# A local attention product split by halves of the queries, and element work moved to ScalarE and GpSimd

## The chip, the cores and the metric

The kernel runs on one core of a Trainium2 chip. Its time is the device time of one execution in microseconds. Five engines work at once and wait for each other by semaphores: TensorE (PE, with its weight loads shown as PEld), VectorE (DVE), ScalarE (ACT), GpSimd (POOL) and SyncE (SP), which issues DMAs.

## What is computed

The reference takes 8 batches of 1024 tokens with 256 features and does, for each batch:

```
h  = layernorm(x) * (1 + scale) + shift                      # adaLN, from the conditioning vector
q,k,v = block-diagonal projections of h (16 heads of 16), q and k rotated
y  = causal softmax(q k^T / 16) v                            # one head of 256 features, 1024 keys
x  = x + gate * y;   u = layernorm(x) * (1 + scale) + shift
for 2 layers:                                                # local transformer
    qkv = shift_token(u) @ wqkv                              # 8 heads of 64
    q,k = l2norm, scale, rotary;  windows of 128 queries look at their own and the last window,
          masked to keys j with i-128 <= j <= i
    u = u + softmax(q k^T * 8) v @ wo
    h = layernorm(shift_token(u)) @ w1 + b1;  u = u + (a * gelu(g)) @ w2 + b2
out = x + gate2 * u
```

## The kernel before, in words

Everything of a batch stays in SBUF. The first attention (pieces `st` to `ys`) works on 8 tiles of 128 tokens; the local layers work on 8 windows `w` of 128 tokens, two layers, so a batch has 16 windows, numbered `n` over all batches (128 in all); the feed-forward part works on two halves `g` of 512 tokens in 5 blocks and a tail of 42 columns.

The work is cut into about 9,000 named pieces. Each engine executes its pieces in an order read from tables: `BEGIN` gives a begin time to each piece of one batch, batch `b` is put `b * PERIOD` later, `EDGE` has other times for the first batch and `ONCE` those of the weight preparation. `schedule()` sorts the pieces of each engine by these times. `plan_banks()` then gives the eight PSUM banks to the pieces in PE's order, and a piece that takes over a bank waits until the piece before has been read out. The begin times set the order and the banks and nothing else: at run time each piece starts when its engine has come to it and its semaphores allow it.

The pieces that the change touches:

- **G** (line 547) are the scores of a window, one piece for each half `f` of the heads: fp32 matmuls with 64 rows of the array and 64 columns (the profile writes 64*64), so that four work at a time.
- **H** (line 565) transposes the probabilities with 64 rows and 128 columns (64*128). The 192 keys of 64 queries lie in `PW` between stretches of 64 zeros; H reads 256 keys for each query, and so the transposed probabilities `PTW` hold two blocks of 64 by 64 zeros for each head. The zeros are written once for each batch, by GpSimd in piece `pz` (lines 1353 and 1354).
- **I** (line 581) is the product with V, one piece for each `f`: for two pairs of heads and for the old and the new 128 keys, two fp32 matmuls side by side, each with 128 rows, 64 columns (128*64) and 128 queries moving. Both keys' halves accumulate in the same place of one bank. Each fp32 matmul is two instructions in the trace, so a piece is 16 of them (8 in the first window of a layer, which has no old keys).
- `oh` (ACT, line 837) and `ol` (DVE, line 1130) copy the product out as two fp16 parts, and **J** (lines 594 and 598) multiplies it by `wo` with the whole array (128*128).
- `rw` (DVE, line 936) applies the first layer norm, `x` minus the mean times the inverse deviation, two tiles at a time; `af` (DVE, line 950) applies scale and shift to the transposed tiles in PSUM; `lk` (DVE, lines 1158 and 1160) is the layer norm before the feed-forward part, four instructions for two windows. Their inverse deviations come from GpSimd: `rt` and `lt` call `root` (lines 294 and 296), an addition and a power.
- `yr` (DVE, line 1183) adds the feed-forward result to `U`; in the last layer it also multiplies by the gate and adds `X` (lines 1188 and 1190), which ends the window. SyncE stores it and loads the next batch's tiles into `X`, after which `st` (line 920) starts the next batch.

Around the change, the largest PE pieces are E (lines 508 and 514, the qkv projection, fp16, 128*128), Wg and Wa (613, 617), Y (160 to 162, 638), the scores and products of the first attention (461, 160 to 162) and the fp32 transposes F (524), D and N (407), pp (419).

Of the kernel before, what the change touches and what calls it, by code (L numbers as in the profile page):

```python
# [22 lines left out]
P = 128  # L23
# [5 lines left out]
AH = 16  # L29
# [17 lines left out]
def adaln_kernel(nc, x, w_q, w_k, w_v, wqkv, q_scale, k_scale, wo, ln_g, ln_b, w1, b1, w2, b2,  # L47
# [3 lines left out]
    with ExitStack() as ctx:  # L51
# [38 lines left out]
        mx1, nm1, sm1, ri1 = (stats[:, 0, :, 16 + i] for i in range(4))  # L90

# [96 lines left out]
        s_pz, s_pa = sem("prob_pads_zero"), sem("odd_probs_normalised")  # L188
# [103 lines left out]
        def root(pool, ve, mv, rs, lo, hi, s_eps, count):  # L292

            pool.tensor_scalar(ve[:, lo:hi], mv[:, lo:hi, 1], EPS, None, ALU.add).then_inc(s_eps, 1)  # L294
            pool.wait_ge(s_eps, count)
            return pool.tensor_tensor(rs[:, lo:hi], ve[:, lo:hi], neg_half[:, 0:hi - lo], ALU.pow)


        block = nc.Block()
        with block:  # L300
# [100 lines left out]
            def _(pe):  # L401
# [9 lines left out]
                for piece in ORDER["pe"]:  # L411
# [141 lines left out]
                    elif k == "H":  # L553
# [3 lines left out]
                        if n % (DEPTH * NT) == 0:  # L557
                            pe.wait_ge(s_pz, n // (DEPTH * NT) + 1)
# [9 lines left out]
                    elif k == "I":  # L568
# [7 lines left out]
                        bk = bank["I", n]  # L576
                        for i in range(2):
# [115 lines left out]
            def _(act):  # L693
                for piece in ORDER["act"]:
                    k, ids = piece[0], piece[1:]
                    if k == "hh":
# [5 lines left out]
                        act.activation(ht[0][:, :, 1 + p * 256:1 + (p + 1) * 256], hf1[:, p % 2], ACT.Copy).then_inc(s_hh, 1)  # L702
                    elif k == "vc":
# [117 lines left out]
                    elif k == "hc":  # L821
                        n, f = ids
                        act.wait_ge(s_ht, at("H", n, f))
                        if n >= 1:
                            act.wait_ge(s_pv, at("I", n - 1, f))
                        c = 1 if n % NT else 2
# [3 lines left out]
                    elif k == "oh":  # L830
# [6 lines left out]
                        act.activation(ot[0][:, :, :], ps[:, bank["I", n], :].rearrange("p (h n) -> p h n", h=4),  # L837
# [75 lines left out]
            def _(dve):  # L913
                for piece in ORDER["dve"]:
# [11 lines left out]
                    elif k == "rw":  # L926
                        b, p = ids
                        dve.wait_ge(s_rstd, at("rt", b, p))
                        if p >= 2:
                            dve.wait_ge(s_xnT, at("pp", b, p - 2))  # L930
                        elif b:
                            for s in range(2):
                                dve.wait_ge(s_ft, at("F", last_n(b), s))
                        for i in range(2):
                            t = 2 * p + i
                            last = dve.tensor_scalar(
                                xn1[:, p % 2, i, :, :].rearrange("p c (h q) -> p (c h) q", q=AD),
                                X[:, t, :].rearrange("p (q h) -> p h q", h=AH),
                                mv1[:, t, 0:1], rs1[:, t:t + 1], ALU.subtract, ALU.mult)
                        last.then_inc(s_xn, 1)  # L940
                    elif k == "af":
                        b, p = ids
                        dve.wait_ge(s_xnT, at("pp", b, p))
                        if p >= 2:
                            dve.wait_ge(s_hl, at("hl", b, p - 2))
                        if b == 0 and p == 0:
                            dve.wait_ge(s_modc, 1)
                        bk = bank["pp", b, p]
                        for c in range(NC):
                            last = dve.tensor_scalar(hf1[:, p % 2, c, :], ps[:, bk, c * 256:(c + 1) * 256],  # L950
                                                     modc_all[:, b, NC + c:NC + c + 1], modc_all[:, b, c:c + 1],
                                                     ALU.mult, ALU.add)
                        last.then_inc(s_hf, 1)
# [134 lines left out]
                    elif k == "tm":  # L1088
# [4 lines left out]
                        dve.wait_ge(s_rinv, at("pw", n))  # L1093
                        if n < 2:
                            dve.wait_ge(s_masks, 1)
# [22 lines left out]
                    elif k == "hv":  # L1118
                        n, f = ids
                        dve.wait_ge(s_ht, at("H", n, f))  # L1120
                        if n >= 1:
                            dve.wait_ge(s_pv, at("I", n - 1, f))
                        c = 1 if n % NT else 2
# [3 lines left out]
                    elif k == "ol":  # L1127
                        n, = ids
                        dve.wait_ge(s_oh, at("oh", n))
                        dve.tensor_tensor(ot[1][:, :, :], ps[:, bank["I", n], :].rearrange("p (h n) -> p h n", h=4),  # L1130
                                          ot[0][:, :, :], ALU.subtract).then_inc(s_ol, 1)
# [19 lines left out]
                    elif k == "lk":  # L1151
                        L, p = ids
                        dve.wait_ge(s_lnr, at("lt", L, p))
                        if L or p >= 2:
                            dve.wait_ge(s_nt, at("N", *divmod(L * 4 + p - 2, 4)))
# [765 lines left out]
```

## Time and profile before

| | us |
|---|---|
| median of 3 timed runs | 2636.95 (2635.13 to 2637.11) |
| span of the profiled execution | 2634.1 |
| PE busy | 2526.7 (96%) |
| DVE busy | 2260.9 (86%) |
| ACT busy | 1935.6 (73%) |
| POOL busy | 1303.7 (49%) |

The profile gives the profiled execution's own time as its span, from the first to the last instruction; the timed runs also hold what lies around the span, some 3 us. A matmul's record lasts until its result is out of the array, so records of matmuls that follow each other overlap, and the distance between their starts is what they cost. A busy PE is therefore not a PE at its peak.

### The profile page before, as it was taken

How to read it: one execution, taken by the hardware profiler on the slowest of the kernel's cores; microseconds unless marked ns; L12 is line 12 of the kernel's file. 1: busy time of each engine (PE TensorE's matmuls, PEld its weight loads, DVE VectorE, ACT ScalarE, POOL GpSimd, SP SyncE). 2: the span in 40 equal slices, each digit the busy share in tenths (PEclk: the TensorE clock that was granted, in tenths of full speed). 3: DMA queues.
4: the chain of work that ended last, by engine and by line, in shares of the span. 5: the costliest groups of instructions: out<-in, count | busy, mean ns of one | idle time of the engine just before them, and what ended most of it. 6: DMA issues, size and time to landing. Idle time of an engine off the chain costs nothing.

```text
span 2634.1 us, 71297 instructions
## 1 busy us (share of the span) xinstructions
PE 2526.7 (96%) x25566; PEld 1725.1 (65%) x25566; DVE 2260.9 (86%) x6247; ACT 1935.6 (73%) x4782; POOL 1303.7 (49%) x953
## 2 busy tenths in 40 slices
PE   7899989999899998999999999999999999999998
PEld 4566666666567665676656666666766666666675
DVE  8997889878898788987889878998889978799785
ACT  3698856888478784788748787587874878658884
POOL 2364535555355554555436554365544555446552
PEclk8999999999999999999999999999999999999999
DMA  5000010000100000000000000000000000000000
GB/s 192 22 7 8 5 43 3 9 5 15 33 3 9 6 17 30 4 10 4 18 29 5 8 5 20 25 6 8 6 19 25 6 8 6 20 25 6 7 6 21
DMA packets 51021, 46.45 MB, mean 18 GB/s; under 512 B 11530, under 2 KB 47980, under 8 KB 50548
## 3 DMA queue, kind: packets, MB, share of 16 engines
q1 hardware_dynamic: 50004, 40.78, 5.0%
q8 instruction: 213, 3.49, 0.6%
q14 instruction: 132, 1.08, 0.1%
q10 hardware_dynamic: 672, 1.10, 0.1%
HBM read 25.06 MB, written 8.42 MB: 13 GB/s over the span
## 4 chain that ended last, share of the span: by engine, by line
PE 69%; DVE 12%; ACT 8%; issue 5%; POOL 4%; DMA 1%; SPq 1%; DVEq 0%; POOLq 0%; ACTq 0%
PE ps L508 10%; PE ps L613 9%; PE ps L581 8%; PE ps L547 6%; PE ps L514 5%; PE ps L617 4%; PE ps L565 4%; PE ps L524 3%; PE ps L594 3%; PE ps L160 2%; PE ps L162 2%; PE ps L161 2%; ACT ar_b L808 2%; PE ps L461 2%; PE ps L407 2%
## 5 line engine op out<-in xcount | busy, mean ns | idle before, releaser
L808 ACT ACTIVATE ar_b<-ar_b,small 128x192 f32<-128x192 f32 (+1 forms) x1024 | 445.2, 437 | 50.4 <-DVE small L1100 48.6
L1366 POOL TENSOR_TENSOR small<-small,neg_half 128x16 f32<-128x16 f32 x128 | 382.2, 2986 | 121.8 <-DVE small L1059 119.9
L1370 POOL TENSOR_TENSOR ar_c<-ar_c 128x1024 f32<-128x1024 f32 x128 | 302.7, 2365 | 282.3 <-DVE ar_c L1086 281.7
L1100 DVE CUSTOM_DVE_ANT_0 ar_b<-ps,mask_t,small 128x192 f32<-128x192 f32 x896 | 319.3, 413 | 29.7 <-PE ps L547 29.2
L1385 POOL TENSOR_TENSOR mlp<-mlp 128x512 f16<-128x512 f32 x160 | 196.3, 1231 | 200.5 <-ACT mlp L863 199.3
L508 PE MATMUL ps<-wqkv_hi,ht_hi 128*128 128x512 f16 x768 | 292.2, 381 | 0.0
L508 PE MATMUL ps<-wqkv_lo,ht_hi 128*128 128x512 f16 x768 | 291.1, 379 | 0.0
L613 PE MATMUL ps<-ht_hi,w_hi 128*128 128x512 f16 (+1 forms) x704 | 268.2, 381 | 5.5 <-ACT ht_hi L759 5.5
L613 PE MATMUL ps<-ht_hi,w_lo 128*128 128x512 f16 (+1 forms) x704 | 267.1, 379 | 0.0
L581 PE MATMUL ps<-ar_b,ar_a 128*64 128x128 f32 x3840 | 239.4, 276 | 0.5 <-DVE ar_b L1124 0.3
L294 POOL TENSOR_SCALAR stats<-stats 128x2 f32<-128x2 f32 x128 | 33.2, 260 | 407.6 <-DVE stats L1149 312.5
L514 PE MATMUL ps<-wqkv_hi,ht_lo 128*128 128x512 f16 x768 | 228.4, 379 | 0.0
L581 PEld LDWEIGHTS ps<-ar_b,ar_a 128*64 128x64 f32 x3840 | 207.2, 137 | 29.7 <-issue 17.4
L617 PE MATMUL ps<-ht_lo,w_hi 128*128 128x512 f16 (+1 forms) x704 | 209.9, 380 | 0.0
L1176 DVE SCALAR_TENSOR_TENSOR mlp<-ps,bias,mlp 128x512 f32<-128x512 f32 x192 | 142.5, 749 | 70.1 <-PE ps L617 33.1
L819 ACT ACTIVATE ar_b<-ar_b,rsw 128x192 f32<-128x192 f32 (+1 forms) x512 | 193.7, 441 | 11.2 <-DVE rsw L1111 10.2
L547 PE MATMUL ps<-ar_a 64*64 64x64 f32 (+2 forms) x5536 | 196.7, 282 | 2.8 <-ACT ar_a L798 2.8
L1124 DVE COPY ar_b<-ps 128x512 f32<-128x512 f32 (+1 forms) x256 | 160.2, 648 | 44.1 <-PE ps L565 44.1
L808 ACT ACTIVATION_READ_ACCUMULATOR ar_b<-ar_b,small 128x1 f32 x1024 | 193.4, 189 | 0.0
L547 PEld LDWEIGHTS ps<-ar_a 64*64 64x64 f32 x5536 | 153.4, 133 | 40.0 <-issue 22.6
L160 PE MATMUL ps<-w_hi,mlp 128*128 128x256 f16 x640 | 175.4, 274 | 0.2 <-POOL mlp L1385 0.2
L162 PE MATMUL ps<-w_hi,mlp 128*128 128x256 f16 x640 | 175.1, 274 | 0.0
(193 smaller groups left out, 6673.3 us busy)
## 6 DMA issues: line engine op xcount, KB each, us to landing
xu<-in_L_attn_x_dram SPq DMA_DIRECT2D x32, 256.0 KB, 2.8
out_dram<-xu SPq DMA_DIRECT2D x64, 128.0 KB, 2.4
rows<-xu SPq DMA_DIRECT2D x128, 63.5 KB
mlp<-in_L_ffn_wqkv_dram SPq DMA_DIRECT2D x2, 1536.0 KB, 6.4
modb<-mod_rows SPq DMA_DIRECT2D x8, 384.0 KB, 4.5
rows<-in_L_ffn_w_dram SPq DMA_DIRECT2D x2, 1364.0 KB, 9.5
rows<-xu SPq DMA_DIRECT2D x112, 0.5 KB
ar_b<-in_L_wmod_dram SPq DMA_DIRECT2D x2, 768.0 KB, 7.4
```

The costliest lines, as they stand in the source:

```text
L160: pe.matmul(o, a[0], b[0], start=start, stop=False)
L162: return pe.matmul(o, a[1], b[0], start=False, stop=stop)
L508: pe.matmul(ps[:, bk, :], ht[0][:, c, a:a + P], wqkv_p[i][:, L % DEPTH, c, s * INNER:(s + 1) * INNER], start=(c == 0 and i == 0), stop=False)
L514: last = pe.matmul(ps[:, bk, :], ht[1][:, c, a:a + P], wqkv_p[0][:, L % DEPTH, c, s * INNER:(s + 1) * INNER], start=False, stop=(c == 1))
L547: last = pe.matmul(ps[HQ * half:HQ * half + HQ, bk[q], i * KW + o:i * KW + o + m], QT[r:r + HQ, n % 2, hp, HQ * half:HQ * half + HQ], KT[r ...
L581: last = pe.matmul(ps[64 * q:64 * q + 64, bk, (h // 2) * P:(h // 2 + 1) * P], V[:, (n - 1 + kb) % 4, h * DH:(h + 1) * DH], PTW[:, f, q, 2 ...
L613: pe.matmul(ps[0:m, bk, :], q[:, L % DEPTH, c, 2 * j + i, 0:m], ht[0][:, c, a:a + 512], start=(c == 0 and q is w1_p[0]), stop=False)
L617: last = pe.matmul(ps[0:m, bk, :], w1_p[0][:, L % DEPTH, c, 2 * j + i, 0:m], ht[1][:, c, a:a + 512], start=False, stop=(c == 1))
L808: last = act.activation(pw, pw, ACT.Exp, bias=mnw[:, n % 2, h:h + 1], scale=-1.0, accum_out=smw[:, n % 2, h:h + 1])
L1100: dve.tensor_tensor_reduce(out=PW[:, pw_at(f, q, i) + c:pw_at(f, q, i) + KW], in0=ps[:, bk, i * KW + c:(i + 1) * KW], in1=mask, scale=rinv ...
L1366: pool.tensor_tensor(rinv[:, n % 4, :], ssm[:, n % 2, :], neg_half[:, 0:16], ALU.pow).then_inc(s_rinv, 1)
L1370: pool.tensor_tensor(M1[:, n % 2, :], M1[:, n % 2, :], M2, ALU.add).then_inc(s_add, 1)
```

## The change

1. **The V product.** Piece I no longer multiplies the zero blocks. Each head's queries are two halves of 64, accumulated in two adjacent banks. For each pair of heads it issues: the old 128 keys for the first half, two matmuls side by side (128 rows, 64 columns, 64 queries moving); the new 128 keys for the second half, two such; and then the remaining 64 keys of each half, four matmuls with 64 rows and 64 columns. In a layer's first window the old keys fall out. `oh` and `ol` read both banks, `plan_banks` gives I two banks, piece `pz` is gone, and the first window's copies `hc` and `hv` wait for the first attention's last product instead, and its `tm` for the last transposes.
2. **Moves.** `rw`, `af` and `lk` run on ScalarE, as one activation for each former DVE instruction, `Identity` with scale and bias from SBUF. For that the mean times the inverse deviation is needed with its sign turned: `rt` and `lt` on GpSimd call `root_bias`, which has two more instructions. The last gate and sum of a batch leave `yr` and become piece `yg` on GpSimd.
3. **Begin times.** All tables are replaced; PERIOD is 318.03 instead of 316.98, and EDGE now holds the first two batches.

```diff
-                            for kb in range(first, 2):
-                                for q in range(2):
-                                    h = 4 * f + q + 2 * i
-                                    last = pe.matmul(ps[64 * q:64 * q + 64, bk, (h // 2) * P:(h // 2 + 1) * P],
-                                                     V[:, (n - 1 + kb) % 4, h * DH:(h + 1) * DH],
-                                                     PTW[:, f, q, 2 * i + kb, :], start=(kb == first),
-                                                     stop=(kb == 1), skip_group_check=True)
+                            o = (2 * f + i) * HQ
+                            heads = [((4 * f + 2 * i + q) * DH, ps[HQ * q:HQ * q + HQ, bk:bk + 2, o:o + HQ]) for q in range(2)]
+                            pt = [PTW[:, f, q, 2 * i:2 * i + 2] for q in range(2)]
+                            if first == 0:
+                                for q, (v, acc) in enumerate(heads):
+                                    pe.matmul(acc[:, 0], V[:, old, v:v + DH], pt[q][:, 0, 0:HQ], start=True, stop=False,
+                                              skip_group_check=True)
+                            for q, (v, acc) in enumerate(heads):
+                                pe.matmul(acc[:, 1], V[:, new, v:v + DH], pt[q][:, 1, HQ:P], start=True, stop=(first == 1),
+                                          skip_group_check=True)
+                            for q, (v, acc) in enumerate(heads):
+                                last = pe.matmul(acc[:, 0], V[0:HQ, new, v:v + DH], pt[q][0:HQ, 1, 0:HQ], start=(first == 1),
+                                                 stop=True, skip_group_check=True)
+                                if first == 0:
+                                    last = pe.matmul(acc[:, 1], V[HQ:P, old, v:v + DH], pt[q][HQ:P, 0, HQ:P], start=False,
+                                                     stop=True, skip_group_check=True)
...
+        def root_bias(pool, ve, mv, rs, nb, lo, hi, s_eps, count):
+
+            pool.tensor_scalar(ve[:, lo:hi], mv[:, lo:hi, 1], EPS, None, ALU.add).then_inc(s_eps, 1)
+            pool.tensor_scalar(nb[:, lo:hi], mv[:, lo:hi, 0], -1.0, None, ALU.mult)
+            pool.wait_ge(s_eps, 2 * count - 1)
+            pool.tensor_tensor(rs[:, lo:hi], ve[:, lo:hi], neg_half[:, 0:hi - lo], ALU.pow).then_inc(s_eps, 1)
+            pool.wait_ge(s_eps, 2 * count)
+            return pool.tensor_tensor(nb[:, lo:hi], nb[:, lo:hi], rs[:, lo:hi], ALU.mult)
...
+                    elif k == "lk":
+                        L, p = ids
+                        act.wait_ge(s_lnr, at("lt", L, p))
...
+                            act.activation(XN[:, p % 2, i, 0:P], U[:, w, 0:P], ACT.Identity, scale=rsl[:, w:w + 1],
+                                           bias=nbw[:, w:w + 1])
...
+                    elif k == "yg":
...
+                        pool.tensor_tensor(U[:, w, :], U[:, w, :], modg[:, :], ALU.mult).then_inc(s_fa, 1)
+                        pool.wait_ge(s_fa, b * NT + w + 1)
+                        pool.tensor_tensor(U[:, w, :], U[:, w, :], X[:, w, :], ALU.add).then_inc(s_fin, 1)
```

## Rows read from the trace of the kernel before

**Rows 1.** the page, parts 1 and 4: the whole kernel.

```profile
span 2634.1 us, 71297 instructions
...
PE 2526.7 (96%) x25566; PEld 1725.1 (65%) x25566; DVE 2260.9 (86%) x6247; ACT 1935.6 (73%) x4782; POOL 1303.7 (49%) x953
...
PE 69%; DVE 12%; ACT 8%; issue 5%; POOL 4%; DMA 1%; SPq 1%; DVEq 0%; POOLq 0%; ACTq 0%
PE ps L508 10%; PE ps L613 9%; PE ps L581 8%; PE ps L547 6%; PE ps L514 5%; PE ps L617 4%; PE ps L565 4%; PE ps L524 3%; PE ps L594 3%; PE ps L160 2%; PE ps L162 2%; PE ps L161 2%; ACT ar_b L808 2%; PE ps L461 2%; PE ps L407 2%
```

**Rows 2.** timeline of PE (start, length): first scores of two batches.

```profile
1006.31 0.50 PE L461 MATMUL ps<-ar_a 128*128 128x128 f16 x6
...
1327.38 0.50 PE L461 MATMUL ps<-ar_a 128*128 128x128 f16 x6
```

**Rows 3.** windows: one batch, busy us of each engine.

```profile
1006.30:1327.40 321.10, 312.05 (x3194) 213.33 (x3193) 277.95 (x773) 239.46 (x595) 162.82 (x118) 0.99 0.05 13
```

**Rows 4.** waits of the whole kernel with PE waiting.

```profile
PE ps L419 <- DVE ar_c L936: 11.9, 16, 3.9
PE ps L407 <- DVE rows L1160: 11.8, 15, 4.6
```

**Rows 5.** timeline of PE in the windows: start, length, form, count.

```profile
1106.00 0.60 PE L524 MATMUL ps<-id_f,ar_c 128*128 128x128 f32 x4
1106.43 0.27 PE L594 MATMUL ps<-wo_hi,rows 128*128 128x256 f16 x1
...
1107.74 0.60 PE L524 MATMUL ps<-id_f,ar_c 128*128 128x128 f32 x4
1108.28 1.23 PE L565 MATMUL ps<-id_f,ar_b 64*128 64x64 f32 x32
1109.44 0.39 PE L508 MATMUL ps<-wqkv_hi,ht_hi 128*128 128x512 f16 x1
...
1110.84 1.57 PE L547 MATMUL ps<-ar_a 64*64 64x128 f32 x64
1112.34 1.97 PE L581 MATMUL ps<-ar_b,ar_a 128*64 128x128 f32 x32
1114.23 0.39 PE L508 MATMUL ps<-wqkv_hi,ht_hi 128*128 128x512 f16 x1
```

**Rows 6.** timeline of PE: a score pair of the 64x192 form.

```profile
1100.64 1.53 PE L547 MATMUL ps<-ar_a 64*64 64x192 f32 x32
1102.10 0.39 PE L508 MATMUL ps<-wqkv_hi,ht_hi 128*128 128x512 f16 x1
```

**Rows 7.** timeline of PEld: the weight load behind that pair.

```profile
1102.10 0.10 PEld L508 LDWEIGHTS ps<-wqkv_hi,ht_hi 128*128 128x128 f16 x1 [0.28 <-issue]
```

**Rows 8.** timeline of PE: around a short wait.

```profile
1310.75 0.27 PE L638 MATMUL ps<-w_hi,rows 128*128 128x256 f16 x1
1310.86 0.27 PE L638 MATMUL ps<-w_lo,rows 128*128 128x256 f16 x1
1311.50 0.33 PE L419 MATMUL ps<-id_f,ar_c 128*128 128x128 f32 x1 [0.37 <-DVE ar_c L936]
```

**Rows 9.** groups by line and form: moved operations and their kin.

```profile
L1158 DVE TENSOR_SCALAR rows<-xu,stats 128x128 f32<-128x128 f32 x128 | 43.9, 343 | 11.7 <-POOL stats L296 11.7
L936 DVE TENSOR_SCALAR ar_c<-xu,stats 128x256 f32<-128x256 f32 x64 | 29.9, 509 | 7.3 <-POOL stats L296 7.3
L819 ACT ACTIVATE ar_b<-ar_b,rsw 128x128 f32<-128x128 f32 x64 | 21.5, 401 | 1.0 <-DVE rsw L1111 1.0
L855 ACT ACT_TABLE_LOAD x56 | 71.8, 1283 | 1.0
L1376 POOL TENSOR_TENSOR ar_c<-ar_c,small 128x512 f32<-128x512 f32 x128 | 137.1, 1071 | 12.8 <-POOL small L1366 0.5
L294 POOL TENSOR_SCALAR stats<-stats 128x2 f32<-128x2 f32 x128 | 33.2, 260 | 407.6 <-DVE stats L1149 312.5 <-DVE stats L924 86.1 <-DVE stats L1025 7.4
```

**Rows 10.** the chain of waits where a batch begins.

```profile
1027.29 0.44 DVE xu L1188
```

More of the change, by code:

```diff
@@ L90, in adaln_kernel @@
         mx1, nm1, sm1, ri1 = (stats[:, 0, :, 16 + i] for i in range(4))
+        nb1, nbw = (stats[:, i, :, 16] for i in (1, 2))
         ar_a = sb("ar_a", [P, 24 * 256])
@@ L702, in _ @@
                         act.activation(ht[0][:, :, 1 + p * 256:1 + (p + 1) * 256], hf1[:, p % 2], ACT.Copy).then_inc(s_hh, 1)
+                    elif k == "rw":
+                        b, p = ids
+                        act.wait_ge(s_rstd, at("rt", b, p))
+                        if p >= 2:
+                            act.wait_ge(s_xnT, at("pp", b, p - 2))
+                        elif b:
+                            for s in range(2):
+                                act.wait_ge(s_ft, at("F", last_n(b), s))
+                        for i in range(2):
+                            t = 2 * p + i
+                            last = act.activation(
+                                xn1[:, p % 2, i, :, :].rearrange("p c (h q) -> p (c h) q", q=AD),
+                                X[:, t, :].rearrange("p (q h) -> p h q", h=AH),
+                                ACT.Identity, scale=rs1[:, t:t + 1], bias=nb1[:, t:t + 1])
+                        last.then_inc(s_xn, 1)
+                    elif k == "af":
+                        b, p = ids
+                        act.wait_ge(s_xnT, at("pp", b, p))
+                        if p >= 2:
+                            act.wait_ge(s_hl, at("hl", b, p - 2))
+                        if b == 0 and p == 0:
+                            act.wait_ge(s_modc, 1)
+                        bk = bank["pp", b, p]
+                        for c in range(NC):
+                            last = act.activation(hf1[:, p % 2, c, :], ps[:, bk, c * 256:(c + 1) * 256], ACT.Identity,
+                                                  scale=modc_all[:, b, NC + c:NC + c + 1], bias=modc_all[:, b, c:c + 1])
+                        last.then_inc(s_hf, 1)
+                    elif k == "lk":
+                        L, p = ids
+                        act.wait_ge(s_lnr, at("lt", L, p))
+                        if L or p >= 2:
+                            act.wait_ge(s_nt, at("N", *divmod(L * 4 + p - 2, 4)))
+                        for i in range(2):
+                            w = 2 * p + i
+                            act.activation(XN[:, p % 2, i, 0:P], U[:, w, 0:P], ACT.Identity, scale=rsl[:, w:w + 1],
+                                           bias=nbw[:, w:w + 1])
+                            last = act.activation(XN[:, p % 2, i, P:DIM], XS[:, w, :], ACT.Identity, scale=rsl[:, w:w + 1],
+                                                  bias=nbw[:, w:w + 1])
+                        last.then_inc(s_xnw, 1)
@@ L925, in _ @@
                         last.then_inc(s_mv, 1)
[L926 to L953, printed above, removed]
                     elif k == "rp":
@@ L1093, in _ @@
                         dve.wait_ge(s_rinv, at("pw", n))
+                        if n % (DEPTH * NT) == 0:
+                            for i in (NT - 2, NT - 1):
+                                dve.wait_ge(s_ptr, at("pt", n // (DEPTH * NT), i, 1))
                         if n < 2:
@@ L1150, in _ @@
                         last.then_inc(s_lnmv, 1)
[L1151 to L1155, printed above, removed]
-                        for i in range(2):
-                            w = 2 * p + i
-                            dve.tensor_scalar(XN[:, p % 2, i, 0:P], U[:, w, 0:P], mvw[:, w, 0:1],
-                                              rsl[:, w:w + 1], ALU.subtract, ALU.mult)
-                            last = dve.tensor_scalar(XN[:, p % 2, i, P:DIM], XS[:, w, :], mvw[:, w, 0:1],
-                                                     rsl[:, w:w + 1], ALU.subtract, ALU.mult)
-                        last.then_inc(s_xnw, 1)
                     elif k == "us":
@@ new lines @@
+    ("dv", "dve"): {(0,): 16.32, (1,): 93.51},
+    ("dw", "dve"): {(0, 0): 19.49, (0, 1): 22.67, (1, 0): 56.41, (1, 1): 84.02},
+    ("z0", "dve"): {(): 0},
+    ("zM", "pe"): {(): 11.79},
+    ("zR", "pe"): {(): 6.21},
+    ("zT", "pe"): {(): 7.71},
+    ("zW", "pe"): {(): 15.29},
+    ("za", "act"): {(): 0},
+    ("zb", "sp"): {(): 10.48},
+    ("zc", "sp"): {(): 0},
+    ("zd", "act"): {(): 7.35},
+    ("ze", "act"): {(): 10.59},
+    ("zf", "dve"): {(0,): 40.65, (1,): 79.59},
+    ("zg", "sp"): {(): 8.48},
@@ new lines @@
+    ("zh", "act"): {(): 12.57},
+    ("zi", "dve"): {(): 11.04},
+    ("zk", "dve"): {(): 8.45},
+    ("zl", "dve"): {(): 13.57},
+    ("zm", "sp"): {(): 27.93},
+    ("zn", "dve"): {(): 15.84},
+    ("zo", "sp"): {(0,): 8, (1,): 3.07},
+    ("zp", "dve"): {(): 7.83},
+    ("zq", "sp"): {(0,): 20.48, (1,): 36.36},
+    ("zr", "act"): {(): 22.52},
+    ("zs", "sp"): {(): 21.13},
+    ("zt", "dve"): {(): 24.77},
+    ("zu", "dve"): {(): 2},
+    ("zv", "sp"): {(0,): 4, (1,): 32.36},
+    ("zw", "sp"): {(0,): 3.55, (1,): 37.01},
```

104 lines of the change are left out of this document (37 added, 67 removed), and 984 rows, old and new, of tables (BEGIN, EDGE).

## The prediction

> **What bounds the kernel.** I read the page first: PE is busy for 96% of the span, DVE for 86%, and the chain that ended last runs 69% through PE, 12% through DVE and 8% through ACT [rows 1]. The chain is spread over many PE lines, line 581 (the V product) with 8%, so the bound is PE's whole queue and not one stage. Then the period: the first score matmuls of two successive batches start 321.1 us apart [rows 2], and within this stretch PE is recorded busy 312.1 us, DVE 278.0, ACT 239.5, POOL 162.8 [rows 3]. PE is thus idle for 9.0 us of a batch. It loses more than that, because a matmul's record reaches past its place in the stream: line 638's two matmuls start at 1310.75 and 1310.86, the next was due 0.11 later again and came at 1311.50, so 0.53 us were lost where the record says 0.37 [rows 8]. The same comparison over all PE starts of the batch gives about 15 us lost, and 306 us of work. What PE waited for longest is DVE's `rw` and `lk`, 11.9 and 11.8 us in the whole kernel [rows 4], 1.5 a batch each. So whatever adds to or takes from PE's 306 us counts nearly in full; freeing other engines can give back no more than 15 us a batch.
>
> **The V product, its stream.** What a matmul costs is the distance of starts. Four fp32 transposes of 128 columns run from 1106.00 to 1106.43, 0.108 us each [rows 5]. The V product of a window is 32 instructions, two side by side, so 16 steps of 128 columns: 1.72 us. After the change a window's steps have 64 columns. Two rows price these. A score pair with 8 steps of 128 and 8 of 64 columns takes 1.50 us (1110.84 to 1112.34), and less 0.86 for the wide ones and 0.17 that I explain below, 0.06 remain for a narrow step with four tiles at a time. The transposes of the probabilities take 1.16 us for 16 narrow steps of two tiles, less the same 0.17: 0.06 again [rows 5]. A half of the heads now needs 8 steps with two tiles side by side (two pairs of heads, old and new keys, two instructions each) and 4 steps with four tiles, 12 x 0.06 = 0.72; a window 1.44 instead of 1.72. In a layer's first window it is 8 steps a half, 0.96 instead of 0.86. A batch: 14 x 0.28 - 2 x 0.10 = 3.7 us less.
>
> **The V product, its changes of form.** The new piece mixes two forms of the array: 128*64 for the whole key blocks, 64*64 for the half blocks, then 128*64 again for the next pair of heads, and 64*64. What does it cost to go from one form to another? The window's V product starts at 1112.34 and the next piece at 1114.23: 1.89 us for 1.72 of stream, so 0.17 more [rows 5]. A score pair of 8 steps of 192 columns (1.29 us) takes 1.46, again 0.17 more [rows 6]. The transposes F take 0.43 us ahead of a full-array piece and 0.54 ahead of the 64*128 form, 0.11 more [rows 5]. The weight load behind the score pair shows why: it was held up 0.28 us, and nothing that it waits for is named [rows 7]; ordinarily it lies under the matmuls before it. Both V product halves are in one form, and so are both score halves, and each pair pays once. So a change of form costs between 0.11 and 0.17 us; I take 0.14, since the rounding of the steps may hold a part of the 0.17.
>
> The Trainium skill, page TensorEngine Tiling (Array Packing), Key Properties, says that changing the tiling mode, and not just the tile, drains TensorE. The trace agrees with the price at the borders of pieces; it has no piece that changes the form inside, and there it is the rule that speaks against this change: by it each half pays three more drains and a batch comes out 14 us heavier for PE; without it the split leaves only the shorter stream (the first rival).
>
> Counting forms in PE's order, as the begin times of one batch give it: before there are 85 changes. In the new order there are 111 between pieces of different forms, 7 places where a V product half follows a half (it ends in 64*64 and the next begins in 128*64), and 3 inside each of 32 halves, 96. That is 214, 129 more: 129 x 0.14 = 18.1 us a batch (14.2 at 0.11, 21.9 at 0.17). With the stream, PE's work grows by 18.1 - 3.7 = 14.4 us (10.5 to 18.2).
>
> **The moves.** DVE loses `lk` (256 instructions, 43.9 us in line 1158 and as much in 1160), `rw` (29.9) and `af` (of the same size, taken at 30), and the last gate and sum, 128 x 0.43 = 55 by the chain's row: some 203 us, 25 a batch, so 278 becomes 253 [rows 9, 10]. ACT gains as many instructions: 256 of 128 columns at 21.5/64 = 0.34 are 86 us, and 128 of 256 columns, bounded by 0.34 below and 0.54 above (line 936 on the slower side for ACT), at 0.42 are 54; 17 a batch. In the new order ACT turns 82 times between exponential and gelu where the old turns 112 times, and a table load is 1.28 us [rows 9]: 5 us a batch less. So 240 becomes 252. POOL gains 128 instructions of 256 columns, near half of line 1376's 1.07 us, 69 us, and 96 times two small ones between 0.26 (line 294) and 0.5, 50 to 96 us, and loses the zeros of `pz`; some 16 a batch, 163 becomes 179 [rows 9]. All three stay far below PE's 320, so none of them enters the sum as busy time; they matter as waits. What is behind them: `lk` waits for `lt`, now 0.5 to 1.0 us longer, and N, Wg and Wa wait for it; ACT's queue behind `lk` and `rw` holds the exponentials, copies of H and E, and these hold banks. On the other side, DVE no longer does `yr`'s 0.87 us three times while the next batch's statistics and `rw` stand behind it (the chain at a batch's beginning goes through just these [rows 10]), and the subtraction that releases the scores comes sooner.
>
> **Stalls.** The 15 us that PE loses today shrink for two reasons: 25 us less on DVE, and a PE with 14 us more work that is late less often to be waited for. Bounds: 3 us remain (at least the beginning of a batch, where each step waits for the one before) or all 15. The V product's longer latency (some 0.35 us a half) and the two banks that it holds speak against the low end. I take the middle, 7.5.
>
> **Sum.** A batch: 321.1 + 14.4 - 7.5 = 328.0, or 6.9 us more. Eight batches (the first and the last share their ends with weights and stores, but do the same V products): 55 us. The profiled execution's span is 2634.1 [rows 1]; it becomes 2689. The runs shown have a median of 2636.95, 2.9 us above the span: 2692 us. The outer bounds: 10.5 - 12 = -1.5 a batch, 2625; and 18.2 - 0 = 18.2 a batch, 2783.
>
> **Rivals.**
>
> *No price inside a piece (faster).* The 0.11 to 0.17 us may belong to the beginning of a piece, its semaphore and its first loads, and not to the form. For it: every case in the trace is a border of pieces. Against it: borders between pieces of one form cost nothing (line 524 after others 0.43 for four), and one price fits three forms. It would give -3.7 + 26 x 0.14 = 0 of work, and the freed DVE would take 3 of the 15 us: -24 us, 2613 us. It decides if the V product half takes under 0.9 us. Chance 17%.
>
> *The stalls stay.* ACT and GpSimd are slower links in the same chains: two more small instructions on POOL before each norm, POOL for the last sum, the norm behind a queue of exponentials. Then 14.4 x 8 = 115: 2752 us. For it: the waits of rows 4 are chains and not lack of DVE time. Chance 15%.
>
> *The stalls nearly vanish.* 3 us remain: +2.4 a batch, 2656 us; with the price of a change at its low bound no difference that could be told. Chance 16%, of which 4 for within 0.2%.
>
> The forecast itself, 2665 to 2725, has 52%. So slower by over 0.2% (5.3 us, about what a measurement here can tell) has 0.78, within it 0.04, faster 0.18 (the first rival and a little of the third). The range holds 8 in 10 from 2620 to 2745: it leaves out half or more of the first rival and the upper part of the second.
>
> **What would show it.** The V product of a window takes 2.4 to 2.8 us from start to start instead of 1.89, with 64*64 and 128*64 rows taking turns and their loads each held up by "issue"; the waits of PE's loads for "issue" at line 581's successor grow from a few to hundreds of times. DVE falls to about 253 us a batch, ACT stands near 252 and POOL near 179. The period is 326 to 331 us. I am wrong if a V product half takes about 0.75 us, or if PE's lost time doesn't fall from 15 us; if the period is below 321, the first of these is the reason.

## The result, and the profile after

The changed kernel takes 2844.61 us (median of 4 runs, 2841.48 to 2848.98), beside it the one before 2637.03 (2635.13 to 2638.8): a ratio of 1.0786 [1.0771, 1.0801], 207.6 us slower. The direction was forecast, the size (+55) was not, and the time lies above the range.

The page of the changed kernel, parts 1 and 4, answers to [rows 1]:

```profile
span 2839.7 us, 79144 instructions
...
PE 2667.3 (94%) x29406; PEld 1778.1 (63%) x29406; DVE 2181.6 (77%) x5735; ACT 2086.7 (73%) x5136; POOL 1466.9 (52%) x1257
...
PE 69%; DVE 8%; issue 5%; POOL 4%; ACT 3%; DMA 2%; DVEq 0%; ACTq 0%; POOLq 0%
```

PE is busy for 140.6 us more than before, but for a smaller share of the span, and the chain runs through PE for the same 69%: both what PE has to do and what it waits for grew. One steady batch, from a first score matmul to the next, beside [rows 2, 3] (columns: window, length, busy PE, PEld, DVE, ACT, POOL, the granted clock as a share of 2.4 GHz, DMA share, GB/s):

```profile
1427.10:1771.50 344.40, 329.59 (x3641) 219.56 (x3640) 266.58 (x708) 257.92 (x638) 183.22 (x157) 0.98 0.04 12
```

The period is 344.0 us as a mean over the steady batches, those between the first and the last, and 320.9 before. The six steady batches make 138 of the 206 us of span; the start up to the first scores makes 13, the first batch 17 and the end behind the last scores 37 (381.5 us instead of 344.2). Start and end go with the new begin times, and not with the product or the moves alone: the first scores come at 46.8 us and the end takes 381.4 us in a3 below, which has neither.

I split the period as the prediction did: for every PE piece the least distance from its first start to the next piece's first start, for its form and its neighbour's, summed over a batch, is PE's *work*; the rest of the period is *lost*. Before: 304.9 of work and 16.0 lost (the prediction had 306 and 15). After: 318.8 and 25.2. Work +13.9, lost +9.2. The split depends a little on how it is made: if each distance between two steps is held against the median of its kind, and only what exceeds it by 0.06 us counts as lost, it is 14.0 lost before and 22.9 after.

A V product half and what follows, PE by start (start, duration of the record, line, operation):

```profile
1405.53 0.34 PE L593 MATMUL ps<-ar_b,ar_a 128*64 128x64 f32 x4
1405.70 0.29 PE L596 MATMUL ps<-ar_b,ar_a 128*64 128x64 f32 x4
1405.91 0.27 PE L599 MATMUL ps<-ar_b,ar_a 64*64 64x64 f32 x1
...
1406.04 0.22 PE L602 MATMUL ps<-ar_b,ar_a 64*64 64x64 f32 x1
1406.19 0.34 PE L593 MATMUL ps<-ar_b,ar_a 128*64 128x64 f32 x4
1406.36 0.29 PE L596 MATMUL ps<-ar_b,ar_a 128*64 128x64 f32 x4
1406.57 0.27 PE L599 MATMUL ps<-ar_b,ar_a 64*64 64x64 f32 x1
...
1406.70 0.22 PE L602 MATMUL ps<-ar_b,ar_a 64*64 64x64 f32 x1
1406.85 0.28 PE L161 MATMUL ps<-w_hi,mlp 128*128 128x256 f16 x1
```

From 1405.53 to 1406.85 are 1.32 us for 0.72 of stream. The last narrow matmul starts at 1406.04 and the next form at 1406.19, 0.15 where a narrow step ordinarily takes 0.06. A half consists of four stretches of one form: three changes inside it and one behind it. Some of the product's weight loads are held up ahead of it as well, with nothing named that they wait for (what PE's loads waited for: us in total, times, longest):

```profile
PEld ps L593 <- issue: 35.0, 120, 0.5
```

That is more than the 17.4 us and 70 times of the product's line 581 before, but not a wait at every change.

And what PE waited for in the whole kernel, beside [rows 4]:

```profile
PE ps L418 <- DVE xu L1073: 22.8, 15, 2.4
PE ps L456 <- POOL ar_c L1369: 22.1, 16, 3.8
PE ps L430 <- ACT ar_c L732: 15.1, 9, 4.9
...
PE ps L418 <- ACT rows L758: 13.9, 4, 10.3
```

Before, no wait was above 12 us; now six are. Two are for the moved norms (`rw`, line 732, and `lk`, line 758), but 10.3 of the 13.9 us for `lk` are one single wait in the last batch, and a3, with `lk` on DVE, has one of 11.8 us at the same place. The two largest are for pieces that the change doesn't touch: `lr` (line 1073, the norm ahead of the local layers, DVE) and `ra` (line 1369, a sum of the first attention's rotation, GpSimd). The kernel before has no wait for `lr`, and this one for `ra`:

```profile
PE ps L445 <- POOL ar_c L1348: 6.0, 8, 1.0
```

In the one steady batch shown above:

```profile
PE ps L418 <- DVE xu L1073: 3.2, 2, 2.4
PE ps L456 <- POOL ar_c L1369: 2.7, 2, 1.9
...
PE ps L430 <- ACT ar_c L732: 1.4, 1, 1.4
```

As a mean of the steady batches PE stands idle for 14.7 us, 9.2 before. The waits for `lr` and `ra` make 5.9 of it (0.8 before), those for the two moved norms 1.5 (2.0 before).

Behind some of these waits the granted clock of TensorE is at the lower of its two levels, 1.2 instead of 2.4 GHz. PE around the longest wait of the batch:

```profile
1516.86 0.65 PE L418 MATMUL ps<-id_f,xu 128*128 128x128 f32 x4 [2.43 <-DVE xu L1073]
...
1517.88 0.63 PE L519 MATMUL ps<-wqkv_hi,ht_hi 128*128 128x512 f16 x1
1518.31 0.63 PE L519 MATMUL ps<-wqkv_lo,ht_hi 128*128 128x512 f16 x1
...
1522.51 0.38 PE L519 MATMUL ps<-wqkv_hi,ht_hi 128*128 128x512 f16 x1
1522.72 0.38 PE L519 MATMUL ps<-wqkv_lo,ht_hi 128*128 128x512 f16 x1
```

```profile
1517.70:1521.10 3.40, 3.40 (x10) 1.22 (x8) 3.25 (x16) 3.40 (x17) 0.00 (x0) 0.50 0.39 120
```

The same pair of matmuls starts 0.43 us apart there and 0.21 later. By the trace's clock records PE is at 1.2 GHz for 10.8 us of a steady batch, 4.6 before. An estimate from the distances of starts within these stretches, against the median of their kind, is that the lower clock lengthens PE's stream by 3.8 us a batch, and by 2.0 before. So some 1.8 of the 9.2 us more of lost time would be the clock.

### The profile page after: what moved, and what is told of

It is laid out like the page before. It is cut to its first block, busy times and chain, and to the rows that moved or that the text cites. A ratio compares the mean times of both kernels' runs of the same rounds, so it can differ in the third digit from the quotient of the medians.

```text
span 2839.7 us, 79144 instructions
## 1 busy us (share of the span) xinstructions
PE 2667.3 (94%) x29406; PEld 1778.1 (63%) x29406; DVE 2181.6 (77%) x5735; ACT 2086.7 (73%) x5136; POOL 1466.9 (52%) x1257
## 4 chain that ended last, share of the span: by engine, by line
PE 69%; DVE 8%; issue 5%; POOL 4%; ACT 3%; DMA 2%; DVEq 0%; ACTq 0%; POOLq 0%
PE ps L519 9%; PE ps L632 8%; PE ps L558 5%; PE ps L574 5%; PE ps L525 4%; PE ps L599 4%; PE ps L636 4%; PE ps L593 4%; PE ps L535 3%; PE ps L613 3%; PE ps L161 3%; PE ps L162 3%; PE ps L163 3%; PE ps L596 2%; PE ps L472 2%
## 5 line engine op out<-in xcount | busy, mean ns | idle before, releaser
L1385 POOL TENSOR_TENSOR ar_c<-ar_c 128x1024 f32<-128x1024 f32 x128 | 310.5, 2426 | 479.2 <-DVE ar_c L1120 478.0
L1381 POOL TENSOR_TENSOR small<-small,neg_half 128x16 f32<-128x16 f32 x128 | 394.4, 3084 | 139.9 <-DVE small L1093 136.9
L1410 POOL TENSOR_TENSOR mlp<-mlp 128x512 f16<-128x512 f32 x160 | 185.5, 1171 | 237.9 <-ACT mlp L925 236.8
L917 ACT ACTIVATE mlp<-ps,bias 128x512 f32<-128x512 f32 x192 | 128.8, 684 | 88.4 <-DVE mlp L1205 50.4
L1154 DVE TENSOR_TENSOR ar_b<-ar_b,rsw 128x384 f32<-128x384 f32 (+1 forms) x256 | 184.0, 719 | 9.0 <-DVE rsw L1148 0.2
L162 PE MATMUL ps<-w_lo,mlp 128*128 128x256 f16 x640 | 175.2, 274 | 0.0
```

The costliest lines, as they stand in the source:

```text
L162: pe.matmul(o, a[0], b[1], start=False, stop=False)
L1381: pool.tensor_tensor(rinv[:, n % 4, :], ssm[:, n % 2, :], neg_half[:, 0:16], ALU.pow).then_inc(s_rinv, 1)
L1385: pool.tensor_tensor(M1[:, n % 2, :], M1[:, n % 2, :], M2, ALU.add).then_inc(s_add, 1)
```

## The experiments

Two theories stood against each other when the work term had been found right. The first: PE's longer work makes it late, and an order fixed for other durations then loses time everywhere. The second, the rival: the moves and the second bank are longer links in chains that PE waits for, whatever its own work. The expectations number a third: the new order itself has longer chains, whatever PE does. The first two exclude each other; the third can hold beside the second. All numbers are in this table, each ratio against the kernel before timed beside it; work and lost are per steady batch, split as above. Where the steady batches of a kernel differ (a2 334.8 to 338.4, a3 341.2 to 345.4), so does its lost time.

| kernel | median us | ratio [95%] | period | work | lost |
|---|---|---|---|---|---|
| before | 2637 to 2641 | | 320.9 | 304.9 | 16.0 |
| after | 2844.61 | 1.0786 [1.0771, 1.0801] | 344.0 | 318.8 | 25.2 |
| a1_old_product | 2777.11 | 1.0524 [1.0508, 1.0539] | 335.0 | 308.4 | 26.6 |
| a2_grouped | 2784.01 | 1.0548 [1.0532, 1.0564] | 336.5 | 309.1 | 26 to 29 |
| a3_order_only | 2838.69 | 1.0749 [1.0730, 1.0768] | 344.4 | 308.4 | 33 to 37 |
| a4_short_product | 2748.03 | 1.0415 [1.0400, 1.0431] | 332.5 | 298.7 | 34 |
| b1_new_product | 2780.83 | 1.0533 [1.0515, 1.0550] | 338.5 | 316.6 | 21.9 |
| b2_moves | 2720.93 | 1.0306 [1.0291, 1.0322] | 331.1 | 304.9 | 26.3 |
| b3_lk | 2699.83 | 1.0227 [1.0206, 1.0248] | 328.2 | 304.9 | 23.3 |
| b4_rw_af | 2663.79 | 1.0091 [1.0076, 1.0106] | 324.6 | 304.9 | 19.7 |
| b5_yg | 2629.84 | 0.9959 [0.9945, 0.9973] | 319.6 | 304.9 | 14.6 |
| b6_root_bias | 2657.86 | 1.0070 [1.0053, 1.0086] | 323.9 | 304.9 | 19 |
| b7_two_banks | 2686.75 | 1.0181 [1.0166, 1.0196] | 327.0 | 304.8 | 22 |
| b9_all_old_order | 2856.94 | 1.0827 [1.0810, 1.0843] | 348.2 | 317.2 | 31.0 |
| b10_banks_apart | 2648.47 | 1.0036 [1.0023, 1.0050] | 322.0 | 304.8 | 17 |
| b11_yg_again | 2628.78 | 0.9962 [0.9948, 0.9975] | 319.6 | 304.9 | 14.8 |

**The product alone, undone (a1) and with fewer changes of form (a2), both in the new order.** Both keep the two adjacent banks reserved. a2 issues the same matmuls in an order in which its sums don't come out as the reference's, so it prices the order and nothing else.

```diff
 # a1: the changed kernel, piece I, oh and ol as before (and the zeros pz)
-    pe.matmul(acc[:, 0], V[:, old, v:v + DH], pt[q][:, 0, 0:HQ], ...)      # and the other three
+    pe.matmul(ps[64 * q:64 * q + 64, bk, (h // 2) * P:(h // 2 + 1) * P], V[...], PTW[:, f, q, 2 * i + kb, :], ...)
 # a2: the changed kernel, the loop over i twice
-for i in range(2): old 128 keys; new 128 keys; the two 64-key parts
+for i in range(2): old 128 keys; new 128 keys
+for i in range(2): the two 64-key parts
```

> The changed kernel with the old V product (zero blocks back, piece pz back on GpSimd just behind the first kk of a batch, the old oh and ol; two banks still set aside), all moves and all new begin times kept. PE's work falls by some 10 us a batch, from 319 to 309. Theory 1 (the new order is laid out for a V product half of about 0.76 us; a PE that is late by 0.55 us each time throws the chains behind it out of step): lost time falls with it, from 26 us a batch to the 16 of the kernel before, period near 324, total 2670 to 2700. Theory 2 (ScalarE and GpSimd as slower links) and theory 3 (the new order has longer chains whatever PE does): only the work goes, 8 x 10 = 80 us, 2760.

> The changed kernel with the V product's matmuls in another order: in each half first the 128-row matmuls of both pairs of heads, then the 64-row ones of both, so that the form changes once inside a half and not three times. If a change costs 0.15 us, a half falls from 1.31 to 1.01 us and the work by 9.7 us a batch. Theory 1: the lost time falls too, some 1.7 us for each us of work, 2844 - 130 = 2715. Theories 2 and 3: 2844 - 78 = 2767. If the price belongs to the pieces' borders, nothing changes.

a1 is 67.5 us faster than the changed kernel, 9.0 a batch: all of it work (-10.4); the lost time is a little higher (26.6 instead of 25.2). a2 has the same streams and two changes fewer in a half, 60.6 us in all; the PE timeline of one half:

```profile
1006.49 0.34 PE L593 MATMUL ps<-ar_b,ar_a 128*64 128x64 f32 x4
1006.66 0.29 PE L596 MATMUL ps<-ar_b,ar_a 128*64 128x64 f32 x4
1006.77 0.29 PE L593 MATMUL ps<-ar_b,ar_a 128*64 128x64 f32 x4
1006.89 0.29 PE L596 MATMUL ps<-ar_b,ar_a 128*64 128x64 f32 x4
1007.11 0.27 PE L603 MATMUL ps<-ar_b,ar_a 64*64 64x64 f32 x1
...
1007.50 0.34 PE L593 MATMUL ps<-ar_b,ar_a 128*64 128x64 f32 x4
```

1.01 us instead of 1.32 for the same matmuls. Over all halves the medians are 1.007 and 1.313, so a change inside a piece costs 0.306 / 2 = 0.153 us, within the 0.11 to 0.17 that it cost between pieces. The page TensorEngine Tiling (Array Packing) of the Trainium skill, Key Properties, says that a change of the mode drains the engine; the trace agrees, also inside a piece, and gives the price.

**The product alone (b1), the moves alone (b2), both in the old order.** Begin times are those of before; a moved piece keeps its time on the new engine.

```diff
 # b1: the kernel before, piece I, oh, ol as in the changed kernel
-uses.append((("I", ids[0]), 1, when["ol", ids[0]]))
+uses.append((("I", ids[0]), 2, when["ol", ids[0]]))
 # b2: the kernel before, rw, af, lk to ACT, root_bias, yg to POOL
+    table["lk", "act"] = table.pop(("lk", "dve"))       # so for rw and af
+    BEGIN["yg", "pool"] = {n: BEGIN["yr", "dve"][n] + 0.4 for n in range(8, 16)}
```

> The kernel before with the new V product alone (two banks, new oh and ol; zeros still written, old begin times, no moves). Work rises by 1.31 x 28 + 1.05 x 4 - 28.9 = 12 us a batch. My forecast's step (a busier PE absorbs waits): 2637 + 45 = 2682. Work in full: 2637 + 95 = 2732. Theory 1 (an order laid out for a shorter product loses more than the work): 2637 + 160 = 2795 or more.

> The kernel before with the moves alone: rw, af and lk on ScalarE, root_bias, the last gate and sum on GpSimd, at the begin times that they had (yg 0.4 behind its yr); old V product and old order otherwise. Theory 2: lost time rises by up to 10 us a batch, 2637 + 80 = 2717. Theories 1 and 3: within 20 us of 2637, faster if the freed VectorE counts.

Both lose, 141 and 82 us. b2 has PE's work unchanged at 304.9, and DVE 20 us a batch emptier than in [rows 3] (PE, PEld, DVE, ACT, POOL):

```profile
1366.40:1697.50 331.10, 312.75 (x3162) 212.60 (x3161) 257.95 (x709) 260.81 (x642) 181.04 (x159) 0.99 0.04 13
```

Still 10.3 us a batch more are lost. What PE waited for there:

```profile
PE ps L430 <- ACT ar_c L724: 33.5, 22, 3.9
PE ps L418 <- ACT rows L750: 25.4, 29, 5.6
PE ps L605 <- ACT ar_b L829: 13.8, 7, 2.0
```

The first two answer to [rows 4]: the same two waits for the same two norms, 23.7 us before, 58.9 now. That is the second theory, and against the first, since nothing made PE late. They are 35 of the 67 us by which PE's idle time grew. The third, which was absent before, is for `ev`, ACT's copy of the qkv projection, which stands in the same queue as the moved norms: ACT's fuller queue has a part in it too. b1 shows a part that neither had in it: 5.9 of its 17.6 us a batch are lost time, on which b7 follows.

**The new order without product and moves (a3), and the new order with a product much shorter (a4).** a3 still reserves the two adjacent banks, and writes its zeros at another place of the order. a4 leaves out the 64-row matmuls, and with them a part of the sum, except in a layer's first window.

```diff
 # a3: the changed kernel with a1's edit, and rw, af, lk, yr as before
 # a4: the changed kernel
                             if first == 0:
                                 pe.matmul(acc[:, 0], ... start=True, stop=True ...)
                             ...
+                            if first == 0:
+                                continue
                             for q, (v, acc) in enumerate(heads):
                                 last = pe.matmul(acc[:, 0], V[0:HQ, new, v:v + DH], ...)
```

> The changed kernel with the old V product and with all moves undone (rw, af, lk and the last gate and sum on VectorE again, root as before), at the new begin times: the new order alone. PE's work 308 us a batch as in a1. Theory 2 (the moves make the 10 us of extra loss): the loss falls from 26.5 to about 16, period 325, total 2777 - 80 = 2697. Theory 3 (the new order does): loss stays at 26, total 2777 or, since VectorE is fuller in an order searched for less, more.

> The changed kernel without the V product's 64-row matmuls (left out, except in a layer's first window), so that a half is 8 narrow steps in one form: 0.61 us, less than the 0.76 that the new begin times leave for it. Work 319 - 19 = 300 us a batch. Theory 1 (the new order loses time because the product comes late): the loss falls from 26 towards 16, 2844 - 232 = 2612. Theory 3 (order and moves lose it whatever the product takes): loss 26 or more, 2844 - 152 = 2692.

a4 was to give back lost time if lateness made it. A half falls to 0.615 us and the work to 298.7, but the lost time rises to 34. With a1 and the changed kernel: halves of 0.61, 1.02 and 1.31 us, lost 34, 26.6 and 25.2. A longer product is thus absorbed in part from 0.61 to 1.02 (work +9.7, lost -7) and hardly from 1.02 to 1.31 (work +10.4, lost -1.4). The first theory falls. a3 is what the third theory forecast (2777 us or more), and not the second alone (2697). The new begin times fit the pieces of the change and not the old ones: without them 33 to 37 us a batch are lost, and this kernel, which of the change has the order and the reserved banks alone, is as slow as the whole change. In the old order the reserved pair costs 6 us a batch (b7); what it costs here was not separated. PE's two longest waits of the changed kernel stand here too, with `ra` and `lr` as they were:

```profile
PE ps L456 <- POOL ar_c L1366: 20.0, 16, 1.9
PE ps L418 <- DVE xu L1052: 18.9, 13, 2.4
```

All five kernels with the new begin times have both (20 to 22 us and 19 to 23 us); with the old ones the first is 4 to 8 us and the second is absent. These two waits come with the new order.

**Which move.** In the old order, one each.

```diff
 # b3: the kernel before, lk on ACT and root_bias in lt
+    act.activation(XN[:, p % 2, i, 0:P], U[:, w, 0:P], ACT.Identity, scale=rsl[:, w:w + 1], bias=nbw[:, w:w + 1])
 # b4: the kernel before, rw and af on ACT and root_bias in rt
 # b5: the kernel before, the last gate and sum as yg on POOL
 # b6: the kernel before, root_bias in rt and lt, its result not used
-    root(pool, vew, mvw, rsl, ...)
+    root_bias(pool, vew, mvw, rsl, nbw, ...)
```

> The kernel before with lk alone on ScalarE (with the longer root_bias for it). Of the 10 us a batch that all moves cost, the trace of b2_moves puts 2.2 on N waiting for lk, against 3.2 on pp waiting for rw: 2639 + 30 = 2669 if the moves add up piece by piece; up to 2700 if it is ScalarE's fuller queue (lk is 256 of its 384 new instructions).

> The kernel before with rw and af alone on ScalarE (root_bias for rw). If the links of the chain at a batch's beginning decide (rw is 2 x 0.76 us there, 2 x 0.40 on VectorE, root_bias 0.5 more): 2639 + 45 = 2684. If it is ScalarE's load: 2639 + 15.

> The kernel before with the last gate and sum alone on GpSimd. It takes 7 us a batch from VectorE and the chain at the batch's end has two instructions of 0.6 us in place of 0.43. If the freed VectorE counts at all it should show here: 2639 - 10. If GpSimd's place in the chain decides: 2639 + 10.

> The kernel before with the longer root_bias on GpSimd alone (its second result not used, rw and lk on VectorE as before). If the 0.8 us that it adds to each norm's chain makes the cost of moving lk (59 us) and rw (23 us): 2640 + 60 or more. If it is ScalarE's part (0.48 for 0.34 us an instruction, and its queue): under 2640 + 20.

`lk` costs 59 us, `rw` and `af` 23, `yg` gains 11 (10 in b11), and the sum, 71, is near b2's 82. Two more tiny GpSimd instructions before each norm, with nothing else changed, cost 19. The `lt` and `lk` at one place of a batch, first in the kernel before (GpSimd, then DVE):

```profile
1119.61 0.22 POOL L294 TENSOR_SCALAR stats<-stats 128x2 f32<-128x2 f32 x1 [3.37 <-DVE stats L1149]
1119.91 0.71 POOL L296 TENSOR_TENSOR stats<-stats,neg_half 128x2 f32<-128x2 f32 x1
```

```profile
1120.66 0.35 DVE L1158 TENSOR_SCALAR rows<-xu,stats 128x128 f32<-128x128 f32 x1
...
1121.43 0.34 DVE L1160 TENSOR_SCALAR rows<-rows,stats 128x128 f32<-128x128 f32 x1
```

and then in b3 (GpSimd, then ACT):

```profile
1470.95 0.22 POOL L302 TENSOR_SCALAR stats<-stats 128x2 f32<-128x2 f32 x1 [3.35 <-DVE stats L1172]
1471.25 0.23 POOL L303 TENSOR_SCALAR stats<-stats 128x2 f32<-128x2 f32 x1
1471.43 0.72 POOL L305 TENSOR_TENSOR stats<-stats,neg_half 128x2 f32<-128x2 f32 x1
1472.23 0.20 POOL L307 TENSOR_TENSOR stats<-stats 128x2 f32<-128x2 f32 x1
```

```profile
1472.46 0.49 ACT L721 ACTIVATE rows<-xu,stats 128x128 f32<-128x128 f32 x1 [0.25 <-POOL stats L307]
...
1473.63 0.48 ACT L723 ACTIVATE rows<-rows,stats 128x128 f32<-128x128 f32 x1
```

From the root's first instruction to the norm's start: 1.05 us before, 1.51 here. From the norm's start to its end: 1.11 (1120.66 to 1121.77) and 1.65 (1472.46 to 1474.11). ACT stood idle and waited for the root, so no queue of exponentials is in this pair. Over all pairs it is the same: root 1.10 to 1.65 us, norm 1.11 to 1.65, and the wait between them unchanged (median 0.04 us). A pair's chain is about 1.1 us longer, and there are 8 pairs a batch, 8.7 us; PE lost 7.3 more. That the two are near each other doesn't show that the chain makes all of it. In b3's steady batches PE's idle time grows by 5.0 us: 1.5 of it are waits for `lk` (1.0 before, 2.5 now), and 2.8 are waits for `ev` and `fc`, ACT's copies, whose queue `lk` now shares (0.4 before, 3.2 now). And b6 lengthens the root alone by the same 0.55 us, 12 times a batch, which makes 6.6, and loses 3.0. The longer chain times its count is thus a bound here, and not the price. For `rw` and `af` I have not separated the longer instruction (0.81 us a record instead of 0.51) from ACT's queue.

**The second bank.** One bank is used, as before; b7 reserves the adjacent one beside it, b10 any other one.

```diff
 # b7
-uses.append((("I", ids[0]), 1, when["ol", ids[0]]))
+uses.append((("I", ids[0]), 2, when["ol", ids[0]]))
 # b10
+uses += [(("I", ids[0], *x), 1, when["ol", ids[0]]) for x in ((), (1,))]
```

> The kernel before with two adjacent banks set aside for the V product and only one used. b1 loses 6 us a batch more than before, and its V products wait 5 us a batch, named DVE's read-out of other banks. If the banks make it: 2640 + 45. If the longer product does: 2640 + 5.

> The kernel before with two single banks set aside for the V product, wherever they are free, and one of them used. Two adjacent ones cost 48 us (b7_two_banks). If the number of banks makes it: 2640 + 45. If that they lie side by side does (the planner must wait for two neighbours to be read out): 2640 + 15.

b7 loses 48 us with the computation unchanged, 6 a batch, which is b1's lost time (22 in both): the longer product itself neither loses nor absorbs any. PE's waits in b7, and the same in b1:

```profile
PE ps L581 <- DVE small L1100: 19.7, 24, 1.1
...
PE ps L581 <- DVE ht_lo L1049: 8.9, 9, 1.1
```

```profile
PE ps L584 <- DVE small L1112: 19.2, 23, 1.1
...
PE ps L584 <- DVE ht_lo L1061: 8.9, 9, 1.1
```

The V product's first line waits for DVE's masked scores, which has nothing to do with its operands: it is the last reader of a bank that the pair needs. Two banks that need not be adjacent cost 10 us. Four fifths of the price are thus adjacency and not the number of banks, in this order and by this planner, which must hand out two neighbours at once. In the changed kernel this wait, for the masked scores, is 0.15 us a steady batch (2.6 in b1 and b7): the new order avoids it. A V product with its two halves in banks apart was not tried.

**The whole change in the old order (b9), and b5 once more with 5 rounds (b11).**

```diff
 # b9: b1 and b2 together
```

> The whole change at the old begin times: new V product and all moves. By the sum of the two parts (141 and 82 us): 2863. The changed kernel with its own begin times has 2845, so the search would be worth 18 us; with the old product it was worth -56 (2777 against 2721). If losses overlap, 2820 and the new times are worth nothing here either.

> The kernel before with the last gate and sum alone on GpSimd, once more and in more rounds: 0.9959 of before was measured, 10 us; it should come again between 8 and 13 us below before if it is one, and is then the one part of the change that pays.

b1 and b2 add up: 141 + 82 = 223 against 218 measured. The new begin times then give 12 us back (2856.94 to 2844.61). In the two profiled executions, 20 us apart, they give 4.3 us in each steady batch and 20 in the first, and take 16 at the start and 10 at the end. b11, the same kernel as b5, beats both kernels, 0.9962 [0.9948, 0.9975], 10 us faster than before: the kernel before with the last gate and sum on GpSimd alone.

## Why the prediction was wrong

- **The V product, its stream and its changes of form: right.** 0.72 + 4 x 0.15 is the 1.31 us measured; PE's work rose by 13.9 us a batch, forecast 14.4, and a window takes 2.6 us, forecast 2.4 to 2.8. The rival without a price inside a piece is rejected by a2.
- **The step that failed is "Stalls".** It let the lost time fall from 15 to 7.5 us a batch, within 3 to 15; it rose from 16 to 25, outside its bounds. Neither of its two reasons held. A DVE with 20 us less to do (b2) went with 10.3 us more lost. A PE with more work absorbed almost nothing: b1, with 11.7 us more work, loses what b7 loses with none more, and from a1 to the changed kernel 10.4 us of work absorbed 1.4. I had shut out a rise although the text itself said that `lk` waits for a longer `lt`.
- **What rose instead.** In the old order the terms are the moves, +10.3 (b2), and the second bank, +5.9 (b1, b7), together +15 (b9). With its own begin times the changed kernel avoids most of both: PE's waits for the moved norms are 1.5 us a steady batch, for the bank 0.15. It pays with waits for `lr` and `ra`, 5.1 us more than before, which all kernels with these begin times have, and, by the estimate above, with 1.8 us of slower clock behind waits. The rest of the 9.2 is spread over smaller waits. The sum treated the begin times as neutral and had no term for them. With 25.2 instead of 7.5 it would have been 321.1 + 14.4 + 10.2 = 345.7 a batch; 344.0 was measured.
- **Eight equal batches** was the smaller slip. Eight times 23.1 us are 185; the measured 206 us of span have 21 more at the start and the end, which come with the new begin times.
- **"None of them enters the sum as busy time"** holds, and misled. DVE, ACT and POOL stayed far below the period, yet their instructions stand in a chain. Both waits of [rows 4] were for exactly the two pieces that were moved to a slower engine: there the longer chain, (0.55 + 0.54) x 8 us for `lk`, was the term to bound the loss with, and busy time was not.
- **The moves' durations.** `lk` on ACT starts every 0.39 us, I took 0.34 for it; DVE starts it every 0.26, where I had counted its 0.34 of record, so that DVE lost 20 us a batch in b2 and not 25, and 11 in the changed kernel. `rw` was bounded by 0.54 and takes 0.81 as a record. POOL came out as forecast, 183 to 179. From the changed kernel's groups (busy us, mean ns, idle before and for whom), `rw`:

```profile
L732 ACT ACTIVATE ar_c<-xu,stats 128x256 f32<-128x256 f32 x64 | 48.7, 810 | 8.6 <-POOL stats L307 8.6
```

- **The table loads** fell from 112 to 82 as counted. No run changes them alone. Of the moves only `yg` gave anything back (1.3 us a batch). Its chain is not shorter on GpSimd; but PE's wait for DVE's `ql`, at the batch's beginning, falls from 10.7 to 5.3 us in the kernel, which fits a DVE that comes to `ql` sooner.
- **The rival "the stalls stay"** had the mechanism of b2, slower links in the same chains, and the wrong price: it put them at no loss beyond the 15 us, where they cost 10 more in the old order. For the changed kernel in its own order it names the wrong waits.

Open: why PE waits for `lr` and `ra` in the new order, and why that order loses 33 to 37 us a batch with the old pieces. Whether a better order exists for the whole change is open too; the two that were run differ by 12 us.

## What to carry to other kernels

When a piece is moved to an engine with time to spare, first look whether the bounding engine's longest waits are for that piece; if so, bound its price by the longer chain times its count (here 7.3 us of 8.7, and 3.0 of 6.6), add what it delays in its new queue, and don't count on spare time elsewhere. Bound a small helper instruction ahead of it in the same way, and price a bank by whether it must be adjacent to another. A new order of the same pieces is a change of its own: give it a term, and read the longest waits of the new trace before naming a cause. A bound on a term that leaves out one sign needs a reason for that sign.

## What the runs showed of the hardware

A change between 128*64 and 64*64 costs 0.153 us also inside one accumulation; three of them in a half, 0.46 us, ate three times what skipping the zero blocks saved (0.14).

DVE's fp32 operations with two inputs in SBUF can stand still while GpSimd works. In the changed kernel `nm` (line 1154, 128x384) takes 0.56 us where no GpSimd instruction is beside it, and this, while `ad` (line 1385) runs (DVE, then POOL):

```profile
1581.94 2.50 DVE L1154 TENSOR_TENSOR ar_b<-ar_b,rsw 128x384 f32<-128x384 f32 x1
```

```profile
1580.76 3.27 POOL L1385 TENSOR_TENSOR ar_c<-ar_c 128x1024 f32<-128x1024 f32 x1 [2.43 <-DVE ar_c L1120]
```

DVE's record ends 0.4 us behind POOL's, which is less than the 0.56 that it takes alone: it stood still and ran when POOL was done. Summed over the kernel the line takes 184.0 us (mean 719 ns), before 158.0 (617):

```profile
L1154 DVE TENSOR_TENSOR ar_b<-ar_b,rsw 128x384 f32<-128x384 f32 (+1 forms) x256 | 184.0, 719 | 9.0 <-DVE rsw L1148 0.2
```

The page SBUF — State Buffer of the Trainium skill, section on the two separate sides, describes this as an exclusive lock between GpSimd and a VectorE operation with two SBUF inputs; the trace agrees. It is a part of why DVE stands at 266.6 us a batch in the changed kernel and at 258.0 in b2, where the order puts fewer of these pairs side by side: there the line's mean is 622 ns.
